# VectorE seeds the causal mask into the scores' PSUM bank; two mask matmuls a step are dropped

## What is computed

```
q, k, v = heads of x @ wq, x @ wk, x @ wv          # x is layer-normed
q, k = rope(rms_norm(q)), rope(rms_norm(k));  k_ctx = rms_norm(ctx @ wk_ctx)
scores = q @ concat(k_ctx, k).T / sqrt(128) + mask  # mask: 0 over the context, -inf where j > i
x = x + tanh(g0) * (softmax(scores) @ concat(v_ctx, v)) @ wo
x = x + tanh(g1) * down(silu(gate(ln(x))) * up(ln(x)))   # e4m3-rounded weights
```

## Time and profile before

| | |
|---|---|
| median of 3 executions | 320.4 us (318.52 to 320.48) |
| the profiled execution: time, span of its core | 318.94 us, 317.1 us |
| busy: PE, PEld | 297.3 us (94%), 232.6 us (73%) |
| busy: DVE, ACT, POOL | 228.2 (72%), 232.3 (73%), 181.3 us (57%) |
| the chain that ended last, by engine | PE 53%, DVE 16%, ACT 16%, issue 6%, POOL 6%, DMA 2% |
| mask matmuls, L635 | 64, 9.6 us busy |
| granted TensorE clock | 0.999 of full |

### The profile page before, as it was taken

The page is one execution under the profiler, slowest core; times in us unless marked ns, Lnnn a source line. Parts: engine busy times, 40 slices in busy tenths (PEclk is TensorE's granted clock), DMA queues, the critical chain, the costliest instruction groups (busy, mean ns, idle before and its releaser), DMA issues.

```text
span 317.1 us, 6533 instructions
## 1 busy us (share of the span) xinstructions
PE 297.3 (94%) x2223; PEld 232.6 (73%) x2223; DVE 228.2 (72%) x478; ACT 232.3 (73%) x892; POOL 181.3 (57%) x177
## 2 busy tenths in 40 slices
PE   7897989999999899999999999999999999898866
PEld 3344656657677688878878888888878888787764
DVE  1668998898769877769886776767764865585454
ACT  2468787877977688897898768877887678776622
POOL 1235685678646875447865685557645685465320
PEclk9999999999999999999999999999999999999999
DMA  6999000000000010000000010000000000000000
GB/s 198 396 388 369 6 17 2 0 1 20 0 2 2 2 33 0 2 2 28 10 0 0 2 36 0 2 1 20 0 3 0 2 18 3 0 2 17 2 7 28
DMA packets 6720, 12.84 MB, mean 40 GB/s; under 512 B 800, under 2 KB 4256, under 8 KB 6688
## 3 DMA queue, kind: packets, MB, share of 16 engines
q1 hardware_dynamic: 6688, 12.43, 11.0%
HBM read 11.38 MB, written 1.05 MB: 39 GB/s over the span
## 4 chain that ended last, share of the span: by engine, by line
PE 53%; DVE 16%; ACT 16%; issue 6%; POOL 6%; DMA 2%; SPq 1%; DVEq 0%; POOLq 0%
PE ps_kv L400 6%; PE ps_attn L676 5%; PE ps_y L447 5%; PE ps_scores L640 5%; ACT probs L865 5%; PE ps_y L442 4%; PE ps_transposed L420 4%; PE ps_q L400 4%; PE ps_probs L420 4%; PE ps_ff L514 4%; ACT squares L707 3%; PE ps_ff L534 3%; PE ps_q L408 3%; PE ps_kv L408 2%; DVE row_max L1134 2%
## 5 line engine op out<-in xcount | busy, mean ns | idle before, releaser
L865 ACT ACTIVATE probs<-ps_scores,exp_bias,q_scale 128x128 f32<-128x128 f32 x128 | 56.9, 455 | 19.3 <-DVE exp_bias L1137 19.3
L1309 POOL TENSOR_TENSOR q_rot<-q_rot,q_sin 128x512 f32<-128x512 f32 x31 | 39.6, 1276 | 19.2 <-DVE q_sin L1007 19.0
L1353 POOL TENSOR_TENSOR probs<-probs,row_inv 128x512 f32<-128x512 f32 x32 | 36.7, 1146 | 19.4 <-DVE row_inv L1187 19.3
L1260 POOL TENSOR_TENSOR q_scale<-ssq_eps,minus_half 128x4 f32<-128x4 f32 x32 | 39.3, 1228 | 9.7 <-DVE ssq_eps L1160 8.8
L1271 POOL TENSOR_TENSOR fuse_lo<-fuse,fuse_hi 128x256 fp32r<-128x256 f32 x21 | 15.4, 732 | 44.9 <-ACT fuse_hi L716 44.9
L707 ACT ACTIVATE squares<-ps_q 128x128 bf16<-128x128 f32 x128 | 33.9, 290 | 6.8 <-PE ps_q L400 3.9
L841 ACT ACTIVATE pt<-ps_probs 128x512 f32<-128x512 f32 x32 | 19.2, 599 | 20.1 <-PE ps_probs L420 20.0
L676 PE MATMUL ps_attn<-pt,values 128*128 128x256 f32 x128 | 33.4, 383 | 0.0
L640 PE MATMUL ps_scores<-kt,qt 128*64 128x128 f32 x512 | 33.3, 273 | 0.0
L1003 DVE TENSOR_TENSOR q_rot<-ps_q,rope 128x512 f32<-128x512 f32 x31 | 21.2, 684 | 14.1 <-ACT squares L707 14.1
L640 PEld LDWEIGHTS ps_scores<-kt,qt 128*64 128x64 f32 x512 | 28.9, 137 | 0.0
(11 more groups left out here) (166 smaller groups left out, 872.5 us busy)
## 6 DMA issues: line engine op xcount, KB each, us to landing
q_raw<-in_wq_dram SPq DMA_DIRECT2D x4, 512.0 KB, 8.5
o_raw<-in_wo_dram SPq DMA_DIRECT2D x4, 512.0 KB, 11.6
ctx_t<-in_ctx_dram SPq DMA_DIRECT2D x8, 128.0 KB, 2.7
out_dram<-x_sb SPq DMA_DIRECT2D x8, 128.0 KB, 1.7
stage<-in_gate_w_dram SPq DMA_DIRECT2D x2, 384.0 KB, 10.3
stage<-in_up_w_dram SPq DMA_DIRECT2D x2, 384.0 KB, 11.3
x_sb<-in_x_dram SPq DMA_DIRECT2D x1, 768.0 KB, 13.3
stage<-in_down_w_dram SPq DMA_DIRECT2D x2, 384.0 KB, 13.2
```

Source lines behind the costliest of these rows:

```text
L865: last = nc.scalar.activation(probs[:, i, :], ps_s[:, i * P:(i + 1) * P], ACT.Exp, bias=exp_bias[:, i:i + 1], scale=q_scale[:, k % 2, i:i ...
L1260: return nc.gpsimd.tensor_tensor(dst, src, minus_half[:, 0:src.shape[1]], ALU.pow)
L1309: nc.gpsimd.tensor_tensor(q_rot[:, :, :], q_rot[:, :, :], q_sin[:, :, :], ALU.add)\
L1353: nc.gpsimd.tensor_tensor(probs[:, :, :], probs[:, :, :], row_inv[:, :].unsqueeze(2).broadcast_to([P, 4, P]), ALU.mult).then_inc(probs_rea ...
```

## The change

The mask is kept as 128 columns in `const` (fp32, zero over the context part, one layout for each half of the partitions), and is no longer cast to bf16; `ident_bf` is gone. A new DVE function `set_mask(s)` copies it, repeated over the four heads, into the bank `ps_scores`. It is issued right behind the reciprocal of each step for the step after it (for step 0 behind `normalize(1)`). PE waits for it (`mask_set`) in place of issuing the two mask matmuls, and all eight score matmuls add onto what DVE has written. The warm-up matmuls, now 8 of 512 columns, go into `ps_scores` and open that bank.

```diff
-C_COS, C_SIN, C_MASK, C_ID, C_ALL = 0, DIM, 2 * DIM, 2 * DIM + LEN, 2 * DIM + LEN + P
+C_COS, C_SIN, C_MASK, C_ID, C_ALL = 0, DIM, 2 * DIM, 2 * DIM + P, 2 * DIM + 2 * P
-WARM_MATMULS, WARM_COLS = 11, 384
+WARM_MATMULS, WARM_COLS = 8, 512
-        mask = sb("mask", [P, LEN], bf16)
-        ident_bf = sb("ident_bf", [P, P], bf16)
+        mask = const[:, C_MASK:C_MASK + P]
...
-                    nc.tensor.matmul(ps_y[:, 0:WARM_COLS], ones_bf[:, 0:P], ones_bf[:, :], start=(i == 0),
-                                     stop=(i == WARM_MATMULS - 1))
+                    last = nc.tensor.matmul(ps_s[:, :], ones_bf[:, 0:P], ones_bf[:, :], start=(i == 0),
+                                            stop=(i == WARM_MATMULS - 1), skip_group_check=True)
+                last.then_inc(scores_open, 1)
...
-                    if isinstance(u, int) and step(u, k) == 0:
-                        pe.wait_ge(tables_ready, 6)
+                    pe.wait_ge(mask_set, step(u, k) + 1)
                     scores = four(ps_s)
-                    for r in range(2):
-                        rows = slice(r * LEN, (r + 1) * LEN)
-                        nc.tensor.matmul(scores[rows, :, rows], ident_bf[:, rows],
-                                         mask[:, :].unsqueeze(1).broadcast_to([P, HPG, LEN]),
-                                         start=True, stop=False, skip_group_check=True)
...
             def tables():
                 dve.wait_ge(const_in, 16)
-                nc.vector.tensor_copy(mask[:, :], const[:, C_MASK:C_MASK + LEN]).then_inc(tables_ready, 1)
-                dve.wait_ge(ident_in, 16)
-                nc.vector.tensor_copy(ident_bf[:, :], ident).then_inc(tables_ready, 1)
...
+            def set_mask(s):
+
+                if s == 0:
+                    dve.wait_ge(const_in, 16)
+                    dve.wait_ge(scores_open, 1)
+                else:
+                    dve.wait_ge(exp_ready, s)
+                nc.vector.tensor_copy(four(ps_s), mask.unsqueeze(1).broadcast_to([P, HPG, P])).then_inc(mask_set, 1)
...
                     nc.vector.reciprocal(row_inv[:, :], row_sum[:, :]).then_inc(inv_ready, 1)
+                    if is_step(u, k + 1):
+                        set_mask(step(u, k + 1))
...
             normalize(1)
+            set_mask(0)
```

## The result

The changed kernel takes 321.73 us (median of 8 executions, 321.55 to 322.55), the kernel before, timed beside it, 319.12 us (8 executions, 318.52 to 320.48). The ratio is 1.0072, with a 95% interval from 1.0052 to 1.0091: 2.3 us slower, at least 1.7 and at most 2.9 (the two medians are 2.6 us apart). That is within 1%, but it is no gain. The profiled executions are 318.94 and 321.78 us, 2.84 us apart.

A forecast was written before the change was run, and what follows sets the result against it. PE's loop and that of ACT and DVE were taken as nearly tied. 318.94 - 0.16 + 1.05 + 1.05 + 0.4 + 0.3 + 0.2 - 2.3 = 319.5 us, 0.5 more; on the 320.4 median, 320.9 us, range 317.2 to 324.6.

The forecast's parts named there:

- steps 3, 4 and 28: Later delays from the copy: 0.3 us for steps 3 and 4 together, 0.2 us at step 28's uncovered `ot_lo`.
- Steps 0, 1 and 2: Copy delays the subtraction behind the reciprocal, partly by losing its turn to POOL's `probs`: 1.05, 1.05 and 0.4 us lost.
- The copy: Each DVE copy of the mask into PSUM takes 0.60 us of DVE's time, 0.35 as lower bound.
- The gain of the pairs: Dropping PE's mask matmul pairs: 18 on the chain at 0.13 us each, 2.3 us gained, 4.1 from above.
- The later tiles: DVE's idle time or POOL's `probs` covers the copy; `xt_lo` starts 0.41 us later but its end does not move.
- VectorE's air is not there: Rival: in six later tiles copies put 0.24 and 0.41 us on the chain, +3.9 us, 324.8 us; chance 0.2.
- Step 5's `xn` ends with POOL's `probs` in any case: Behind step 5's reciprocal: `xn` is held by POOL's `probs` anyway, so no loss was booked there.
- PE's waits for `mask_set` cost nothing: Ahead of the scores: the copy is done more than a microsecond before them, so PE's wait costs nothing.
- The start: Two bf16 casts go, gaining 0.24 us; the larger constants load costs 0.08 us; net gain 0.16 us.
- PE is the bound: Rival: PE busy 34.69 of 35 us, so all 32 pairs count at 0.23 us, 315.9 us; chance 0.13.
- the copy is short: Rival: copy takes 0.35 us without trading turns with POOL, steps 0 and 1 cost 0.7 us, 318.8 us; chance 0.12.
- It does nothing: Rival: PE waits for `qt` where the pairs stood, so only the losses remain, 2.8 us, 323.2 us; chance 0.1.

The follow-up runs named there:

- with the pairs gone: The kernel before without its mask matmuls and without any copy, the mask left out of the scores: 318.61 us, ratio 0.9977.
- with the pairs kept: The kernel before with its mask matmuls kept and 31 copies of the same size added behind the reciprocals: 322.96 us, ratio 1.0107.

## Why the prediction was right in the time, and where its steps failed

The forecast was 0.5 us more in the profiled execution, and 320.9 us; it became 2.84 us more, and 321.73 us. The sign, the class of a change under 1% and the range held. The sum did not: its losses were nearly right, its gain was four times too large.

Two strokes of luck hid this in the time. The 320.9 us stood on 320.4, the median of three executions of the kernel before; eight have a median of 319.12, and 0.5 on top of that would have been 319.6, 2.1 us short. And the losses of 3.0 us come near the 3.37 that came in part by chance: 0.5 of them (steps 3, 4 and 28) did not come, and 0.77 (steps 6 and 15) were not foreseen.

**Steps 0, 1 and 2: right, in size and mechanism.** 1.05, 1.05 and 0.4 us were forecast, 1.04, 1.02 and 0.54 came. The subtraction was to take 1.4 to 1.9 us behind a `probs` of 1.04; it takes 1.44, and ends at 28.00 us, where 27.96 was worked out. The chain reaches PE's first long stretch at 48.98 us for 46.33, 2.65 us later (2.3 forecast). Moving the copy by one instruction separates the parts, 0.48 us of DVE time and 0.56 us of the turn. The Trainium skill ("SBUF — State Buffer", on who interferes with whom) says that a DVE instruction with two SBUF inputs contends with GpSimd's reads, and that the second one waits until the first is done. The rows agree: whichever of L945 and `probs` starts first keeps its own duration, 0.96 or 1.04 us, and the other takes 1.44 or 1.72.

**The copy: right.** 0.67 us, the next start 0.58 to 0.60 behind.

**The gain of the pairs: the term that was mis-sized.** "18 x 0.13 = 2.3 us" should have been 11 x 0.08 = 0.9 us, measured as 0.7 us in time with the pairs gone, and as 0.57 us in this kernel. Two factors were wrong. The 0.13 us was the distance from the pair's start to the scores' start; the right distance is that from the pair to what stands *behind* the scores, with and without it, and it is 0.07 to 0.08 us. The trace of before showed only one side of that; since no row gave the price without the pair, the term should have had nothing as its lower bound. "The gap ahead of the pair ... stays" was not quite so: the first score matmul now comes without a 64-wide instruction ahead of it and takes 0.05 us more. And the 18 came from counting a group's presence in the chain. The text had noted itself that the two loops "are close to a tie", and did not apply it: where two loops are tied, a piece taken from one of them gives only until the other is reached. "The reciprocals of one tile after another should then come 0.2 to 0.3 us closer than 35 us apart": from step 17 to step 21 they are 34.91 us apart for 34.96, which is 0.05 us closer.

**The later tiles: right, and by the named cover.** The end of `xt_lo` was not to move. After, at step 19:

```profile
201.06 0.18 DVE L1188 RECIPROCAL row_inv<-row_sum 128x4 f32<-128x4 f32 x1 [1.85 <-ACT probs L860]
201.16 0.67 DVE L979 COPY ps_scores<-const 128x512 f32<-128x512 f32 x1
201.74 0.90 DVE L1197 TENSOR_TENSOR xt_lo<-ctx_t,xt_hi 128x256 fp32r<-128x256 f32 x1
202.57 0.68 DVE L1050 TENSOR_TENSOR ot_lo<-ps_attn,ot_hi 128x512 fp32r<-128x512 f32 x1
...
210.65 0.69 DVE L1050 TENSOR_TENSOR ot_lo<-ps_attn,ot_hi 128x512 fp32r<-128x512 f32 x1 [0.21 <-ACT ot_hi L773]
```

It ends 1.58 us behind the start of the reciprocal, as in the earlier trace rows (198.05 to 199.63), shrunk from 1.27 to 0.90 us; 0.85 was forecast. The idle time ahead of `ot_lo` at j = 1 went from 0.88 to 0.21 us. The rival "VectorE's air is not there" was wrong by one copy: the doubled one shows that the next would have cost.

**What was missed.** Step 15's 0.44 us. I judged all steps of one j by one tile, but behind the reciprocal of step 14 the weight part `o_lo` had kept DVE until the reciprocal itself, and `ot_lo` had no idle time. Now the copy stands there:

```profile
155.73 1.83 DVE L920 TENSOR_TENSOR o_lo<-o_raw,o_hi 128x1024 fp32r<-128x1024 f32 x1
157.49 0.16 DVE L1188 RECIPROCAL row_inv<-row_sum 128x4 f32<-128x4 f32 x1
157.58 0.67 DVE L979 COPY ps_scores<-const 128x512 f32<-128x512 f32 x1
158.16 0.67 DVE L1050 TENSOR_TENSOR ot_lo<-ps_attn,ot_hi 128x512 fp32r<-128x512 f32 x1
```

and PE's output projection, which came without a wait before, waits for it, which the prediction had named as a sign of being wrong:

```profile
158.97 0.35 PE L447 MATMUL ps_y<-o_hi,ot_hi 128*128 128x256 f32 x1 [0.46 <-DVE ot_lo L1050]
```

Then step 6's 0.33 us: "Step 5's `xn` ends with POOL's `probs` in any case" was right for one instruction and forgot the one ahead of it. For steps 3 and 4, where I had put 0.3 us, the reciprocals show nothing (2.65 and 2.65, then 2.60). Nor did the 0.2 us of the `ot_lo` at 284.06 come, which stands behind the reciprocal of step 29: with the pairs kept `ot_lo` starts 0.67 us behind that reciprocal for 0.49, but the `xn` behind it ends 1.89 us behind for 1.90, and the next reciprocals keep their place. The 0.16 us that step 28 lost with the pairs kept is another matter: PE's attention matmuls already end 0.16 us later, measured from the reciprocal of step 27. What held them was not followed further. "PE's waits for `mask_set` cost nothing" holds, but not for the reason given: at steps 1 and 3 the copy is not done more than a microsecond ahead of the scores, it is what PE waits for.

```profile
26.80 1.09 PE L635 MATMUL ps_scores<-kt,qt 128*64 128x128 f32 x16 [0.54 <-DVE ps_scores L979]
```

**The start.** The tables start at 9.55 for 9.69, 0.14 us earlier, where 0.16 was forecast, and 0.13 of it is still there when PE transposes the first queries (17.34 for 17.47). But the projection `ps_q` behind them starts at 18.03 for 17.98, and the first reciprocal comes 0.05 us later. The gain was there and did not reach the first step's end; what the projection waited for the rows don't show.

**The other rivals.** "PE is the bound" and "the copy is short" are refuted by the pairs' 0.7 us and the copy's 0.67 us. "It does nothing" was the nearest to what came: 2.8 us more were said, 2.84 came, but as 3.4 us of losses less 0.57 of gain. And its reason, a wait for the queries (`qt`) at each pair, is not what the rows show: the gain is cut off by the loop of ACT and DVE.

## What to carry to other kernels

A group's share of the chain says where to look, not what its removal gives: in a near tie each piece gives its distance in issue, not its passage, and only until the other loop is reached; measure the distance to the instruction behind it. Work moved to an engine with 30% of idle time is free only where it isn't put between a release and a waiting instruction, so look at every step at which it is inserted, not at one of each kind. And where two engines hold each other up, it is the order of their starts that sets who is late: a move of one instruction was worth 0.56 us a step. A mixture (matmuls where DVE is full, copies where PE is) beat both pure kernels, the kernel before by 0.8 us of 319.

## What was not expected of the hardware

Two things in PE's first 36 us come and go between executions. The first is seen across kernels whose code is the same up to there. In the profile of before the first four projection passes take 1.98 us; with the pairs gone they take this:

```profile
6.16 3.78 PE L408 MATMUL ps_kv<-kv_raw,ctx_t 128*128 128x512 f32 x4 [0.55 <-DMA kv_raw<-in_wk_ctx_dram]
```

Nearly twice as long, though the granted clock of that stretch reads 1.00 and the eleven warm-up matmuls ahead of it took 3.70 us in both. It is seen in four of the ten profiles (3.69 to 3.78 us), three of the four with eleven warm-up matmuls and one of the six with eight, too few to say whether the form matters, and puts the first reciprocal 0.57 to 0.88 us later. The other is shown by the clock. Windows of the kernel with the pairs gone (length, busy us of PE, PEld, DVE, ACT, POOL, then the clock):

```profile
30.00:32.00 2.00, 1.27 (x5) 1.04 (x6) 2.00 (x4) 1.10 (x3) 0.05 (x1) 0.75 0.63 222
32.00:34.00 2.00, 2.00 (x4) 0.68 (x3) 1.93 (x5) 1.09 (x4) 1.82 (x2) 0.50 0.00 0
34.00:36.00 2.00, 2.00 (x11) 1.54 (x10) 1.97 (x4) 1.44 (x7) 1.11 (x2) 0.90 0.01 4
```

The clock falls to 0.50 of full, the 1.2 GHz level, behind a stretch in which PE had waited 1.32 us for DVE's `k_sin`, and four passes that take 1.88 us at 2.4 GHz take this:

```profile
31.43 3.37 PE L408 MATMUL ps_kv<-kv_raw,xt_raw 128*128 128x512 f32 x4
```

It costs 0.54 us by the reciprocal of step 2 (+0.89 at step 1, +1.43 at step 2). Such a wait is not enough for it: in the profile of the changed kernel PE is busy for only 1.07 of the 2 us from 30 to 32, and the clock reads 1.00 throughout. In the profile with late double copies, which up to step 15 is the changed kernel, the clock falls to 0.50 as well, and no reciprocal comes later for it (+2.16 us at step 2 for +2.11): DVE sets the pace there. The falls go together with two groups of times that several kernels here have: of the twelve executions with pairs in the first four steps and the old warm-up, the eight from 319.06 to 319.79 us have, but for one, a mean clock of 0.999 to 1.000, the four from 320.43 to 320.68 us one of 0.993 to 0.995. In the changed kernel clocks of 0.993 and 1.000 lie side by side between 321.55 and 321.86 us. Why one execution falls and the next doesn't stays open; the warm-up's form is not the cause, since with pairs in the first four steps five of twelve executions have a mean clock of 0.993 to 0.995 with either form.
